# Attention's values and sums of weights in one set of 64x32 products, with the second pass in a new order

## The reference, cut to what matters

```
x = x + autocorrelation(layernorm(x), ctx)          # pass one
x = x + layernorm(x) @ (W + lora)                   # pass one
x = x + attention(layernorm(x), ctx)                # pass two, touched here
x = x + ffn(layernorm(x))                           # pass two

# attention: 32 query heads of 16, 8 key/value heads, 4 queries share one
Q = query @ Wq + bq;  K = key @ Wk + bk;  V = value @ Wv + bv
w = softmax((Q K^T) / 4);  y = w V;  out = y @ Wo + bo

# ffn
h = relu(t @ up)^2;  shared = h @ down
routed = (t @ fc1 @ expert @ fc2) * sum(top2(t @ gate))
out = layernorm(shared + routed) * gamma + beta
```

## Time and profile before

| | |
|---|---|
| median of 3 runs | 686.14 us |
| profiled execution | 687.42 us, its span 685.6 us |
| PE busy | 654.6 us (95%) |
| DVE busy | 511.4 us (75%) |
| ACT busy | 432.0 us (63%) |
| POOL busy | 378.5 us (55%) |
| granted TensorE clock | 0.999 |

### The profile page before, as it was taken

One profiled execution on the slowest core, in us unless ns is written; L12 is line 12 of the kernel. 1 busy time (PEld: TensorE's weight loads), 2 busy tenths in 40 slices (PEclk: granted clock), 3 DMA queues, 4 the chain that ended last, 5 costly groups with the idle time before them and its releaser, 6 DMA issues.

```text
span 685.6 us, 12653 instructions
## 1 busy us (share of the span) xinstructions
PE 654.6 (95%) x3964; PEld 482.3 (70%) x3964; DVE 511.4 (75%) x1140; ACT 432.0 (63%) x793; POOL 378.5 (55%) x464
## 2 busy tenths in 40 slices
PE   7889999999999898999999999999999999998986
PEld 3455666666656476788778787887878878786775
DVE  4999998999975877777677677776777767775444
ACT  4788888888746785574655846658367474674221
POOL 1388999888775534435455354554454545535351
PEclk9999999999999999999999999999999999999999
DMA  8334434352126321121212312113021221211000
GB/s 269 121 109 124 139 123 124 123 180 98 62 94 173 117 79 33 46 64 61 63 35 57 90 33 61 45 49 90 31 61 54 69 61 31 61 31 47 17 16 31
DMA packets 32551, 54.37 MB, mean 79 GB/s; under 512 B 5344, under 2 KB 7136, under 8 KB 32512
## 3 DMA queue, kind: packets, MB, share of 16 engines
q1 hardware_dynamic: 32512, 53.90, 26.6%
HBM read 36.84 MB, written 8.39 MB: 66 GB/s over the span
## 4 chain that ended last, share of the span: by engine, by line
PE 78%; DVE 11%; issue 4%; DMA 3%; ACT 3%; POOL 1%; SPq 0%; POOLq 0%; DVEq 0%; ACTq 0%
PE ps_b L1295 8%; PE ps_b L1297 7%; PE ps_b L1296 7%; PE wide L1295 7%; PE wide L1297 6%; PE wide L1296 6%; PE ps_b L1496 4%; PE ps_a L1340 4%; PE bank L1432 3%; DMA ctx_t<-in_ctx 3%; PE wide L1422 3%; PE ps_b L1350 3%; PE ps_a L1295 2%; PE ps_a L1297 2%; PE wide L1550 2%
## 5 line engine op out<-in xcount | busy, mean ns | idle before, releaser
L780 POOL TENSOR_TENSOR va<-mv,small 128x1 f32<-128x1 f32 x80 | 15.3, 192 | 149.0 <-DVE mv L1274 79.5
L745 ACT ACTIVATE stage<-wide 128x512 f32<-128x512 f32 x30 | 16.3, 595 | 83.8 <-PE bank L1597 83.7
L868 POOL TENSOR_TENSOR y_l<-y,y_h 128x512 fp32r<-128x512 f32 x16 | 21.9, 1370 | 72.5 <-ACT y_h L653 72.5
L1142 DVE RECIPROCAL y<-ps_b 128x256 f32<-128x256 f32 x32 | 55.9, 1748 | 0.4 <-PE ps_b L1496 0.4
L676 ACT ACTIVATE probs<-wide 128x1024 f32<-128x1024 f32 x32 | 32.8, 1025 | 36.1 <-PE wide L1550 36.1
L1295 PE MATMUL wide<-up_h,t_h 128*128 128x512 f32 x128 | 52.1, 407 | 1.5 <-DVE t_l L1226 1.5
L1297 PE MATMUL wide<-up_h,t_l 128*128 128x512 f32 x128 | 50.9, 398 | 0.0
L1296 PE MATMUL wide<-up_l,t_h 128*128 128x512 f32 x128 | 50.4, 394 | 0.0
L1295 PE MATMUL ps_b<-down_h,ht_h 128*128 128x512 f32 x120 | 49.6, 413 | 0.4 <-DVE ht_l L1214 0.4
L782 POOL TENSOR_TENSOR rs<-va,small 128x1 f32<-128x1 f32 x80 | 44.5, 557 | 6.3
L1297 PE MATMUL ps_b<-down_h,ht_l 128*128 128x512 f32 x120 | 47.2, 393 | 0.0
(11 more groups left out here) (244 smaller groups left out, 2155.9 us busy)
## 6 DMA issues: line engine op xcount, KB each, us to landing
q_stack<-qt_h SPq DMA_DIRECT2D x128, 64.0 KB, 2.0
ctx_t<-in_ctx SPq DMA_DIRECT2D x16, 256.0 KB, 2.7
x_res<-in_x SPq DMA_DIRECT2D x16, 256.0 KB, 2.9
x_in<-x_rows SPq DMA_DIRECT2D x16, 256.0 KB, 2.7
ctx_t<-in_ctx_turned SPq DMA_DIRECT2D x16, 256.0 KB, 2.9
x_res<-x_rows SPq DMA_DIRECT2D x16, 256.0 KB, 2.9
out<-stage SPq DMA_DIRECT2D x15, 256.0 KB, 3.0
x_in<-in_x SPq DMA_DIRECT2D x8, 256.0 KB, 3.0
```

Of the source, the lines that this page charges most:

```text
L1142: dve.reciprocal(y[:, :, b, :], part[:, 1]).then_inc(S["den_s"], 1)
```

## The change

- `attend` no longer uses ones of its own. `vbd` is filled with 1.0 instead of 0.0 outside the values, and each product takes 64 rows (one head h of a pair) by 32 columns: 16 columns are that head's weighted values, the other 16 its sums of weights. Head h goes to bank 2+h, sequence b to its half. That is 16 products per tile instead of 32.
- Values and sums now lie on different partitions. `attended_out` on ScalarE copies both banks to `sums` (in the place of `x_h`, `x_l`) and head 0's values, masked, to `y`; `numerators` on VectorE adds head 1's. `denominators` on SyncE moves the sums to their partitions in `den` by eight DMAs of 16 partitions; `inverted` takes the reciprocal in SBUF in two halves; `attended` multiplies.
- SyncE's order becomes `load2`, `residual`, `denominators`, store of the output, `stacked`.
- The order of pass two is new on all engines, as are `turn_two`'s. On TensorE: ..., `turned_hidden` 0, `attend`, up, `rough_scores` 0, `turned_hidden` 1, `down` 0, first routed part, `rough_scores` 1, `down` 1, `turned_norm`, `output`, `turned_maxima`, second routed part, `products_kv`, `scores` 0, `queries`, `scores` 1. A new `attend_ready` waits for both weights ahead of `turned_hidden` 0. `output` takes the products with the high half of `y` first and waits for the low half after them.

```diff
@@ SyncE
+            def denominators(t):
+                if live(t):
+                    sp.wait_ge(S["sums_s"], 2 * t + 1)
+                    wait(sp, S["wo_ps"], t)
+                    for h in range(2):
+                        for p in range(PAIRS):
+                            at, beside = STACK * p + HD * h, STACK * p + HD * (1 - h)
+                            sp.dma_start(den[at:at + HD], sums[h][beside:beside + HD]).then_inc(S["den_in"], 16)
             def turn_two():
+                denominators(0)
                 stacked(1)
             def body2(i):
                 load2(i + 4)
-                stacked(i + 3)
                 residual(i + 2)
+                denominators(i + 2)
...
+                stacked(i + 3)
@@ ScalarE
+            def attended_out(t):
+                if live(t):
+                    act.wait_ge(S["pv_ps"], 2 * t + 2)
+                    act.wait_ge(S["qy_ps"], capped(1, t + 2))
+                    for h in range(2):
+                        last = act.activation(sums[h][:].rearrange("p g b q -> p b g q"),
+                                              bank[2 + h].rearrange("p (b g q) -> p b g q", b=2, g=GROUPS), ACT.Copy)
+                    last.then_inc(S["sums_s"], 1)
+                    wait(act, S["wo_ps"], t)
+                    act.activation(y[:].rearrange("p g b q -> p b g q"),
+                                   bank[2].rearrange("p (b g q) -> p b g q", b=2, g=GROUPS), ACT.Copy, scale=place[0]
+                                   ).then_inc(S["sums_s"], 1)
@@ turn_two: attended_out(0) after turned_high(1); y_high(0) after guard_rows(1)
@@ body2: attended_out(i + 2) after hidden_high(i, 0)
...
-                y_high(i + 2)
-                queries_stacked(i + 3)
...  (relu, hidden_high(i, 1))
+                queries_stacked(i + 3)
+                y_high(i + 2)
+                query_high(i + 4)
                 if opening(i):
-                    guard_rows(2)
-                    query_high(3)
                     down_high(1)
-                else:
-                    query_high(i + 4)
-                    guard_rows(i + 3)
+                guard_rows(i + 3)
@@ GpSimd: y_low(i + 2) and the rstd of tile i + 2 after the square; in turn_two after keys_spread(1)
@@ VectorE
-            dve.memset(vbd[:], 0.0).then_inc(S["vbd_zero"], 1)
+            dve.memset(vbd[:], 1.0).then_inc(S["vbd_zero"], 1)
+            def numerators(t):
+                if live(t):
+                    dve.wait_ge(S["sums_s"], 2 * t + 2)
+                    dve.scalar_tensor_tensor(y[:], sums[1][:], place[1], y[:], ALU.mult, ALU.add).then_inc(S["den_s"], 1)
+            def inverted(t, b):
+                if live(t):
+                    dve.wait_ge(S["den_in"], DEN_MOVES * (t + 1))
+                    dve.reciprocal(den[:, :, b, :], den[:, :, b, :]).then_inc(S["den_s"], 1)
             def attended(t):
                 if live(t):
-                    wait(dve, S["wo_ps"], t)
-                    for b in range(2):
-                        part = bank[2 + b].rearrange("p (n g q) -> p n g q", n=2, g=GROUPS)
-                        dve.wait_ge(S["pv_ps"], 2 * t + b + 1)
-                        dve.reciprocal(y[:, :, b, :], part[:, 1]).then_inc(S["den_s"], 1)
-                        dve.wait_ge(S["den_s"], 2 * t + b + 1)
-                        dve.tensor_tensor(y[:, :, b, :], part[:, 0], y[:, :, b, :], ALU.mult).then_inc(S["y_s"], 1)
+                    dve.wait_ge(S["den_s"], 3 * t + 3)
+                    dve.tensor_tensor(y[:], y[:], den[:], ALU.mult).then_inc(S["y_s"], 1)
@@ turn_two: numerators(0), merged_low(0), maxima(1, 0), context_low(2), merged_low(1), maxima(1, 1), normalised(2),
@@   merged_low(2), inverted(0, 0), inverted(0, 1), attended(0), merged_low(3), norm_low(2), values(1), third(0),
@@   keys_biased(2), third_norm(0), queries(2)
@@ body2 after hidden_low(i, 0): numerators(i+2), [down_low(0) at i = -1], context_low(i+4), normalised(i+4),
@@   maxima(i+3, 0), inverted(i+2, 0), hidden_low(i, 1), inverted(i+2, 1), attended(i+2), maxima(i+3, 1), top two
@@   and their sum, norm_low(i+4), values(i+3), [down_low(1) at i = -1], third(i+2), ffn's sum and statistics of
@@   tile i, keys_biased(i+4), third_norm(i+2), queries(i+4)
@@ TensorE
+            def attend_ready(t):
+                if live(t):
                     pe.wait_ge(S["vbd_s"], t + 1)
                     wait(pe, S["kv_s"], capped(1, t + 2))
                     wait(pe, S["z_s"], t - 2)
+                    pe.wait_ge(S["probs_s"], 2 * t + 2)
             def attend(t):
                 if live(t):
                     for b in range(2):
-                        pe.wait_ge(S["probs_s"], 2 * t + b + 1)
-                        for n in range(2):
-                            for p in range(PAIRS):
-                                lhs = ones_bd if n else vbd[:, b, p].rearrange("k h d -> k (h d)")
-                                last = pe.matmul(bank[2 + b][32 * p:32 * (p + 1), 256 * n:256 * (n + 1)], lhs,
-                                                 probs[:, b, p, :], start=True, stop=True)
+                        for p in range(PAIRS):
+                            for h in range(2):
+                                k = slice(SEQ * h, SEQ * (h + 1))
+                                last = pe.matmul(bank[2 + h][STACK * p:STACK * (p + 1), HALF * b:HALF * (b + 1)],
+                                                 vbd[k, b, p].rearrange("k h d -> k (h d)"), probs[k, b, p, :],
+                                                 start=True, stop=True)
                         last.then_inc(S["pv_ps"], 1)
@@ turn_two: attend(0) ahead of merge(0); output(0) and products_kv(2) after scores(1, 0)
@@ turned_hidden: waits for ht_lo; body2: the order given above
```

More of the change, by code:

```diff
@@ L157, in build @@
         x_in, ctx_t = sb("x_in", [P, D]), sb("ctx_t", [P, D])
+        with ExitStack() as tmp:
+            sums = [sb(f"sums{h}", [P, GROUPS, 2, SEQ], stack=tmp) for h in range(2)]
         x_h, x_l = sb("x_h", [P, D], F32R), sb("x_l", [P, D], F32R)
@@ L1193, in turn_two @@
                 queries_low(1)
[L1194 removed]
+                numerators(0)
                 merged_low(0)
@@ L1233, in body2 @@
                     hidden_low(t, 0)
-                attended(i + 2)
+                numerators(i + 2)
                 if opening(i):
                     down_low(0)
+                context_low(i + 4)
+                normalised(i + 4)
+                maxima(i + 3, 0)
+                inverted(i + 2, 0)
+                t = i
+                if live(t) and not final(t):
+                    hidden_low(t, 1)
+                inverted(i + 2, 1)
+                attended(i + 2)
+                maxima(i + 3, 1)
                 t = i + 1
@@ L1519, in output @@
                 if live(t):
+                    pe.wait_ge(S["y_hi"], t + 1)
+                    for g in range(GROUPS):
+                        pe.matmul(bank[2], cols(y_h, g, P), cols(wo_h, g, D), start=(g == 0), stop=False)
+                        pe.matmul(bank[2], cols(y_h, g, P), cols(wo_l, g, D), start=False, stop=False)
                     pe.wait_ge(S["y_lo"], t + 1)
                     for g in range(GROUPS):
[L1522 to L1523 removed]
+                        last = pe.matmul(bank[2], cols(y_l, g, P), cols(wo_h, g, D), start=False, stop=(g == GROUPS - 1))
                     last.then_inc(S["wo_ps"], 1)
@@ L1588, in turn_two @@
                 scores(1, 0)
+                output(0)
+                products_kv(2)
                 queries(2)
@@ L1640, in body2 @@
                 if live(t) and not final(t):
-                    wait(pe, S["y_s"], capped(2, t + 3))
+                    turned_hidden(t, 1)
+                    wait(pe, S["sums_s"], capped(2, t + 3))
                     down(t, 0)
-                output(i + 2)
-                t = i
-                if live(t) and not final(t):
-                    turned_hidden(t, 1)
-                rough_scores(i + 3, 1)
                 t = i + 1
                 if live(t):
-                    wait(pe, S["x3_s"], capped(1, t + 2))
-                    routed_part(t, 0, HALF, bank[2][:, HALF:])
-                if opening(i):
-                    turned_maxima(2)
-                    keys_values(3)
-                else:
-                    keys_values(i + 4)
-                    turned_maxima(i + 3)
+                    routed_part(t, HALF, D + EXPERTS, bank[4])
+                rough_scores(i + 3, 1)
                 if closing(i):
@@ L1662, in body2 @@
                     down(t, 1)
+                turned_norm(i + 4)
+                output(i + 2)
+                turned_maxima(i + 3)
+                t = i + 1
+                if live(t):
+                    wait(pe, S["x3_s"], capped(1, t + 2))
+                    routed_part(t, 0, HALF, bank[2][:, HALF:])
+                products_kv(i + 4)
                 if closing(i):
```

81 lines of the change are left out of this document (41 added, 40 removed).

## The result

The changed kernel takes 698.36 us (median of 4 runs, 697.48 to 701.16), the kernel before 686.0 beside it (4 runs, 685.78 to 686.7): ratio 1.0185, 95% interval 1.0156 to 1.0215. It is slower, as forecast, by 12.4 us where 8.2 were forecast: inside the stated range of 684.5 to 704, and 0.4 above the 690 to 698 that the forecast called its own. Its profiled execution took 698.23 us with a span of 696.4, and its granted clock is 0.987 on the mean, where before showed 0.999.

What follows compares the result with a forecast made beforehand. It took TensorE's queue to bound full turns (78% of the chain), and chains to its products elsewhere. Full turns -1.5, turn into pass two +4.0, turn -1 +5.0, end +0.7: +8.2 on 686.14 gives 694.3 us, range 684.5 to 704.

Steps and rivals of the forecast that it cites:

- Part one: `attend`'s products: half the instructions, row halves and column strips running beside each other, -0.93 us a tile (bounds 0 to -0.93).
- Rival B: The row halves don't overlap within 32-column strips: 16 x 0.93 = +15, so 709 us; chance 0.08.
- Part two: New wait ahead of `attend`: both weights must be there before `turned_hidden` 0, +0.15 us.
- Part three: `output` moves behind three things, to 17.35 into the turn; TensorE then idles 0.6 us for `x3` every turn.
- Part four: `y` and `down` 1's low half arrive in time, 0.2 to spare; GpSimd blocks `numerators` to 6.7; turns total -1.5 us.
- A full turn: One of twelve loop turns, 27.95 us against 28.08: twelve times -0.13 = -1.5 (bounds -6 to +5 in all).
- Part six: Turn -1: little TensorE work hides VectorE's chain to `x3`, so 30.7 us against 25.6: +5 (bounds +2 and +7).
- Part five: Turn into pass two: `output(0)` waits for more VectorE and ScalarE work, so turn -1 begins later: +4.0 (bounds +1 and +6).
- Part seven: The end: turn 12 -1, turn 13 +2.2 from lost cover, last stretch saves some 0.5: +0.7 (bounds -1 and +3).
- Rival A: Faster: the opening turns cost only 2 together and full turns keep 0.45 each: -2.7, 683.4 us; chance 0.17.
- Rival C: `y` comes late in every turn, all twelve paying 0.5 to 0.9: +6 to +10 more, 700 to 704 us; chance 0.2.
- Rival D: Nothing measurable: gains of -8 in full turns meet the opening's +9; chance 0.05.

Runs made afterwards that it cites:

- e4: The changed kernel's order on all engines, but with the old products, sums and reciprocals from PSUM, without copies or moves of sums: 709.58 us, ratio 1.0345.
- e3: The changed kernel with the second routed part written to bank 5, so that it no longer waits for `x3`: 693.07 us, ratio 1.012.
- e1: The changed kernel with dummy products that nobody reads where TensorE newly waits, 19 in `turn_two` and 25 in turn -1: 698.1 us, ratio 1.0171.
- e11: The combined kernel e7 with every dummy product taken out; bank, down halves and two queues remain: 691.05 us, ratio 1.0081.
- e5: The changed kernel with the dummy products of e1 and 16 more in turns 12 and 13 and before the last tile's transposes: 696.13 us, ratio 1.0144.
- e8: The change's products, copies, moves and reciprocals in the loop order of the kernel before, `turn_two` as changed: 783.3 us, ratio 1.1414.
- e7: The changed kernel with e3's bank, later VectorE down halves, turn -1's moves on two queues, and dummy products in opening and end: 683.65 us, ratio 0.9968.
- e6: The changed kernel with VectorE's down halves behind the norm and, in turn -1, four of eight moves issued by ScalarE: 696.28 us, ratio 1.0157.
- e10: e7 with ScalarE's context half ahead of its issues, `y_h` ahead of query rows, and VectorE's second down half moved to turn 0: 690.17 us, ratio 1.0051.
- e12: e7 with ScalarE's context half ahead of its issues, `y_h` ahead of query rows, and 18 dummy products, not 8, ahead of `output(1)`: 684.47 us, ratio 0.9978.

## Why the prediction was right, and where it was off

- **Part one** held: 1.02 in place of 1.86, and 0.83 a tile with the order held the same (e4); its "half the instructions" was a miscount that its sum did not use. Rival B, that the halves of the rows don't overlap, is refuted.
- **Part two** was too small: `attend` starts 2.02 into the turn where it started at 1.68, +0.34 and not +0.15.
- **Part three** held: 0.59 of waiting for `x3` in each full turn, `output` 17.51 into it. e3 took the wait away and got 0.6 a turn back.
- **Part four** held. `y_h` ends 17.0 into the turn (forecast 17.3), and VectorE's `numerators`, two SBUF operands beside GpSimd's `residual_bias`, was blocked. The loop turn of the kernel after, DVE and then POOL:

```profile
453.64 1.61 DVE L1177 SCALAR_TENSOR_TENSOR y<-sums,small,y 128x512 f32<-128x512 f32 x1 [0.75 <-ACT y L676]
```
```profile
453.39 1.30 POOL L904 TENSOR_TENSOR x_res<-x_res,bo_all 128x512 f32<-128x512 f32 x1
```

  It ends at 455.25, 6.55 into the turn (forecast 6.7). In turn -1, with GpSimd already through, it takes 0.75. So the blocking the other way round, which the trace of before did not show, is there, as the Trainium skill says in SBUF — State Buffer, section Who interferes with whom. The eight moves are issued in 4.9 to 5.8 us and land 2.0 later; the reciprocal from SBUF takes 1.74, as from PSUM.
- **A full turn** is 27.97 against 27.95. That it came out this close is in part luck: `attend` gave 0.09 less than forecast and part two cost 0.19 more, but the 0.15 of waiting ahead of `down` 1 does not show (its low half is done at 462.68, `down` 1 starts at 462.99). The twelve came to -0.8, not -1.5; one of them took 28.52.
- **Part six** held, 30.2 against 30.7, and link by link: normalising took 2.16 beside GpSimd's key spread, 2.1 was forecast. The clock fell behind the waits here too (0.50 from 267 to 271) and cost nothing more, since the down half bound `x3`: filled (e1), the turn takes the same 30.2. e4, at 29.9 without moves, shows that the new places made most of it.
- **Part five is the step that was mis-sized**: "Behind the output's start stand 2.56 + 1.19". `output(0)` began where it was forecast, but those 3.75 became 6.36, because TensorE's granted clock went to 0.52 behind its idle time. The forecast priced idle time at its own length only; the clock is in none of its terms. e1 and e11 show it: fills alone give 2.4 us of that stretch back.
- **Part seven** was off the same way, 2.6 against 0.7: turn 13 grew by 2.0 as forecast (+2.2), turn 12 gave 0.4 and not 1, and the rest, from which 0.5 was to be saved, took 1.05 more, at a clock of 0.66 from 667.1 to 672.1. Where the clock stayed up it takes 29.3 to 29.4, 0.5 under before: in e5 with fills, but in e4 and e11 without any in it. So this loss, too, differs from one execution to the next, as does turn 13's, which pays 2.7 on top in e1.
- **Rival A** fell: the opening cost 11. **Rival C** fell for this order, and is what happens in the old one (e8). **Rival D** fell with the opening's 11.

## What to carry to other kernels

Where TensorE is to wait for some microseconds, price the wait twice: its own length, and what the products behind it can cost at half the clock; and see whether harmless products can fill it (here worth 7.4 us in all, e11 against e7). A gain in a loop (0.1 to 0.7 a turn) is soon eaten by the turns at its ends, where there is less work to hide the same chain, so give those an order and a budget of their own. When an issue or a step is moved to another engine to shorten a chain, first look at what is next in that engine's queue (e6, e10, e12).

## What the hardware showed that was not expected

- With PE busy for 3.00 and 1.62 of two stretches of 5 us, the granted clock fell to 0.80 and 0.52, and the float32r products of 512 columns came every 0.43 us in place of 0.23. At 3.17 to 3.19 of 5 us it fell in one kernel's execution and not in another's, and at 2.52 of 5 (e11, 655 to 660) it did not fall. What decides it is not shown.
- The reciprocal of 128x256 float32 takes 1.74 us from SBUF and 1.75 from PSUM.
- Four moves of 16 partitions take SyncE 2.42 us to issue, 0.60 each, and ScalarE 2.72, 0.68 each, behind which ScalarE's next computing step came 2.28 late (e6).
- Sixteen float32 products of 64 rows by 32 columns, 256 wide, take 1.02 us, as many of 128 rows 1.86: two row halves in two banks and four column strips ran beside each other.
